# A causal attention's row maxima: the mask added by an identity matmul on TensorE instead of inside VectorE's reduction

## What is computed

```python
att = jnp.einsum('bhtd,bhsd->bhts', q, k) * scale
causal = jnp.tril(jnp.ones((T, T), dtype=bool))
att = jnp.where(causal, att, jnp.finfo(att.dtype).min)
att = jax.nn.softmax(att, axis=-1)
y = jnp.einsum('bhts,bhsd->bhtd', att, v)
```

## Time and profile before

| what | value |
|---|---|
| median of 3 runs | 748.03 us |
| lowest, highest | 746.31, 754.69 us |
| span of the profiled execution | 748.4 us |
| prologue of the causal attention | 287 to 317 us |
| its loop of eight steps | 317 to 622 us |
| last mixture of experts | 622 to 748.4 us |

### The profile page before, as it was taken

How to read it: one execution, slowest core, us unless ns; L and a number is a source line. 1 busy time by engine, 2 the same in 40 slices (tenths; PEclk the granted TensorE clock), 3 DMA queues, 4 the chain that set the end, 5 groups by cost and what they waited for, 6 DMA issues and landing times.

```text
span 748.4 us, 11770 instructions
## 1 busy us (share of the span) xinstructions
PE 666.3 (89%) x4108; PEld 456.7 (61%) x4108; DVE 501.7 (67%) x1560; ACT 356.8 (48%) x728; POOL 159.1 (21%) x290
## 2 busy tenths in 40 slices
PE   1875767899997997799998899999999997999998
PEld 1664656677776775465555555565555545777775
DVE  3578874776676648977665667769877425666654
ACT  3744355212222464166677678665666673222221
POOL 4563544330002430002433420203020000000000
PEclk9999989989999996799999999999999999999999
DMA  8000000000000000000000000000000000000000
GB/s 293 2 0 1 1 0 1 2 1 1 0 1 1 0 2 1 0 1 1 1 2 1 1 2 1 1 1 2 1 1 2 1 1 1 1 15 1 15 15 14
DMA packets 5722, 7.27 MB, mean 10 GB/s; under 512 B 416, under 2 KB 4640, under 8 KB 5664
## 3 DMA queue, kind: packets, MB, share of 16 engines
q1 hardware_dynamic: 4944, 4.59, 1.9%
q10 hardware_dynamic: 720, 1.93, 0.8%
HBM read 5.47 MB, written 1.05 MB: 9 GB/s over the span
## 4 chain that ended last, share of the span: by engine, by line
PE 70%; DVE 11%; ACT 4%; issue 3%; POOL 2%; POOLq 0%; ACTq 0%; DVEq 0%
PE bank L1568 12%; PE bank L1466 10%; PE bank L1596 10%; PE bank L1526 9%; PE bank L1251 6%; PE bank L1253 5%; PE bank L1252 5%; PE bank L1449 3%; PE bank L1578 2%; DVE hn L862 2%; DVE bank L1134 1%; DVE work L1137 1%; PE bank L1536 1%; PE bank L1259 1%; PE bank L1507 1%
## 5 line engine op out<-in xcount | busy, mean ns | idle before, releaser
L771 ACT ACTIVATE arena<-bank 128x512 f32<-128x512 f32 (+3 forms) x384 | 167.1, 493 | 88.7 <-PE bank L1578 65.1
L1134 DVE CUSTOM_DVE_ANT_0 bank<-bank,mask_qk 128x512 f32<-128x512 f32 (+3 forms) x256 | 121.2, 511 | 48.6 <-PE bank L1596 47.7
L1596 PE MATMUL bank<-kza,qta 128*128 128x512 f32 (+3 forms) x320 | 127.0, 410 | 5.7 <-DVE work L1134 2.0
L698 ACT ACTIVATE work<-bank 128x512 f32<-128x512 f32 x80 | 47.6, 597 | 171.7 <-PE bank L1449 171.7
L1568 PE MATMUL bank<-qtb,kza 128*128 128x512 f32 (+3 forms) x320 | 120.3, 388 | 2.0 <-ACT arena L771 1.0
L1061 DVE TENSOR_TENSOR work<-work,bank 128x512 f32<-128x512 f32 x80 | 54.9, 687 | 82.7 <-ACT work L698 82.2
L1137 DVE TENSOR_REDUCE work<-bank 128x1 f32<-128x512 f32 x128 | 81.6, 684 | 24.4 <-PE bank L1596 23.7
L1568 PEld LDWEIGHTS bank<-qtb,kza 128*128 128x128 f32 x320 | 60.5, 192 | 57.8 <-ACT arena L771 52.1
L1466 PE MATMUL bank<-dw,work 128*128 128x128 f32 x640 | 92.0, 288 | 0.1
L1466 PEld LDWEIGHTS bank<-dw,work 128*128 128x128 f32 x640 | 79.5, 195 | 11.5 <-issue 10.4
L1526 PE MATMUL bank<-arena 128*9 128x512 f32 (+3 forms) x768 | 80.1, 489 | 0.4 <-ACT arena L771 0.4
(11 more groups left out here) (200 smaller groups left out, 1166.0 us busy)
## 6 DMA issues: line engine op xcount, KB each, us to landing
x<-x_in SPq DMA_DIRECT2D x4, 256.0 KB, 10.1
y_out<-x SPq DMA_DIRECT2D x4, 256.0 KB, 2.3
arena<-const_in ACTq DMA_DIRECT2D x1, 976.0 KB, 8.0
arena<-gw_in SPq DMA_DIRECT2D x1, 640.0 KB, 9.2
arena<-uw_in SPq DMA_DIRECT2D x1, 640.0 KB, 8.4
dw<-dw_in SPq DMA_DIRECT2D x1, 640.0 KB, 9.4
work<-q_in SPq DMA_DIRECT2D x2, 256.0 KB, 6.9
arena<-wa_in ACTq DMA_DIRECT2D x1, 393.0 KB, 8.5
```

The costliest lines, as they stand in the source:

```text
L771: act.activation(pb[:, blk % 2, h, 0:w], s_bank(n)[:, 0:w], ACT.Exp, scale=SCALE).then_inc(p_ready, 1)
L1134: ins = dve.tensor_tensor_reduce(out=src, in0=src, in1=mask_qk[:, CW - w:], scale=1.0, scalar=-3e38, op0=ALU.add, op1=ALU.max, accum_out=dst)
L1596: pe.matmul(a_bank(n)[:, 0:w], qta[:, slot(b, g), i * P:(i + 1) * P], kz(s, h, half)[:, 0:w], start=True, stop=True).then_inc(a_full, 1)
```

## The change

Three edits. `mask_qk` shrinks from 512 columns (384 zeros and the triangle) to the 128 of the triangle, and the POOL memset of the zeros goes. On TensorE every masked `score_max` is followed by an identity matmul that accumulates `mask_qk` on the last 128 columns of the bank, and `a_full` is raised by that one. On VectorE all 384 maxima are a plain `tensor_reduce`.

```diff
-        mask_qk = sb("mask_qk", [P, CW], BF16)
+        mask_qk = sb("mask_qk", [P, P], BF16)
...
-            pool.memset(mask_qk[:, 0:CW - P], 0.0)
-            pool.tensor_copy(mask_qk[:, CW - P:], raw_c[:, C_MA:C_MA + P])
+            pool.tensor_copy(mask_qk[:, :], raw_c[:, C_MA:C_MA + P])
...
-                    if i * P < half * CW + w:
-
-                        ins = dve.tensor_tensor_reduce(out=src, in0=src, in1=mask_qk[:, CW - w:], scale=1.0,
-                                                       scalar=-3e38, op0=ALU.add, op1=ALU.max, accum_out=dst)
-                    else:
-                        ins = dve.tensor_reduce(dst, src, AX.X, ALU.max)
-                    ins.then_inc(a_free, 1)
+                    dve.tensor_reduce(dst, src, AX.X, ALU.max).then_inc(a_free, 1)
...
-                    pe.matmul(a_bank(n)[:, 0:w], qta[:, slot(b, g), i * P:(i + 1) * P],
-                              kz(s, h, half)[:, 0:w], start=True, stop=True).then_inc(a_full, 1)
+                    ins = pe.matmul(a_bank(n)[:, 0:w], qta[:, slot(b, g), i * P:(i + 1) * P],
+                                    kz(s, h, half)[:, 0:w], start=True, stop=True)
+                    if i * P < half * CW + w:
+                        ins = pe.matmul(a_bank(n)[:, w - P:w], identb[:, :], mask_qk[:, :], start=False, stop=True,
+                                        skip_group_check=True)
+                    ins.then_inc(a_full, 1)
```

## The result

The changed kernel takes 768.9 us (median of 4 runs, 767.45 to 770.26), the kernel before 747.17 us (median of 4, 745.78 to 754.69). The ratio is 1.0267, with a 95% interval of 1.0214 to 1.032. The forecast was 769.4 us, in a range of 761 to 777.

What follows compares the result with a forecast made beforehand. The prediction took DVE to bound the prologue and PE the loop. From 748.4 us it added 22.4 for masks on PE and took off 1 for gaps and 0.4 for the prologue: 769.4 us, range 761 to 777.

Steps and rivals of the forecast that it cites:

- The bound: Causal attention: DVE bounds the prologue (busy 29.55 of 30.00 us), PE the loop (292.59 of 305 us).
- The gain on DVE in the prologue: Plain instead of masked reductions gain about 0.05 us per maximum, 32 x 0.05 = 1.6 us in the prologue.
- the slope: Reductions on DVE fall 0.13 us per 128 columns, giving plain ones of 0.60, 0.47, 0.34 and 0.21 us.
- what PE would give back there: Prologue: added masks on PE at low clock offset DVE's 1.6 us gain; sum taken as -0.4 us.
- The bound of +2.9 us: Prologue's upper limit: PE at its low clock becomes the bound, and two runs of four blocks lose 2.9 us.
- Rival (d): Prologue: PE's denser work keeps or brings the higher clock, saving 2.6 us, time 766.8 us; chance 0.07.
- The price of a mask: Loop, PE: 0.12 us alone, 0.08 at 128 columns, 0.07 ahead of the sums; 22.4 us over seven steps.
- Rival (c): Each added mask on PE costs its whole row, 0.23 us, so 51.5 us more, about 798 us; chance 0.03.
- What falls in gaps: Loop: added matmuls fill PE's waits for exponentials and a maximum; 1 us taken off, between 0 and 12.4.
- The sum: Whole kernel: 748.4 + 22.4 - 1 - 0.4 = 769.4 us.
- (a): Loop: masks fall into PE's 12.4 us of idle time, leaving 10 us more, time 758 us; chance 0.05.
- (b): DVE sets the pace and shorter reductions pay everywhere, 12.8 us less, time 735.6 us; chance 0.02.

Runs made afterwards that it cites:

- e1: Changed kernel with TensorE's added masks kept but VectorE's old masked reduction put back (mask added twice): 770.22 us, ratio to before 1.0211.
- e2: Changed kernel with plain reductions but no mask for the maxima on either engine, second-pass masks zero (not causal): 748.25 us, ratio to before 0.9929.
- e8: The changed kernel repeated unchanged, with more rounds, beside the kernel before: 769.83 against 750.9 us, ratio 1.0237.
- e0: The kernel before, unchanged, profiled once more: median of one run 754.36 us, span 752.5 us.
- e7: Kernel before with the changed way only in the loop and the old way in the prologue: 775.82 us, ratio 1.029.
- e3: Changed kernel with each added identity matmul issued twice in a row: 777.93 us, ratio to before 1.0319.
- e6: Kernel before with the changed way only for the prologue's 32 masked maxima, the old way in the loop: 751.63 us, ratio 0.9993.
- e9: From e6, the second pass's third mask moved behind the score for the maxima, next to the sums: 750.01 us, ratio to before 0.9983.
- e5: Changed kernel with the added mask matmul streaming 256 columns instead of 128 where the block is wide enough: 771.37 us, ratio to before 1.0247.

## Why the prediction was right

**The bound.** Right for the loop. e1 and e2 part the change: the loop's cost comes with TensorE's matmuls and stays whether VectorE is relieved or not. VectorE's share was not quite nothing, 1.1 us in steps 1 to 6 (e2).

For the prologue it was right only in part. DVE is busy 29.55 of 30 us there, and yet the chain of the kernel before passes over PE for the scores of the first 12 maxima:

```profile
289.99 1.98 PE bank L1596 x3
...
292.02 2.04 PE bank L1596 x4
```

In the changed kernel it stays on DVE:

```profile
290.04 5.55 DVE work L1131 x12
```

The difference is the clock. The windows of the kernel before, of the changed kernel, and of the changed kernel again (e8):

```profile
292.00:297.00 5.00, 4.35 (x13) 3.14 (x13) 4.85 (x21) 1.40 (x3) 0.00 (x0) 0.50 0.00 0
...
293.00:298.00 5.00, 4.26 (x25) 3.14 (x24) 4.97 (x15) 1.36 (x3) 0.00 (x0) 0.99 0.00 0
...
293.00:298.00 5.00, 4.74 (x22) 3.86 (x22) 4.43 (x13) 1.44 (x3) 0.00 (x0) 0.50 0.00 0
```

**The gain on DVE in the prologue.** The 0.05 us a maximum, and the slope by which I had guessed the narrow reductions, hold. The chain of the changed kernel has the last twelve, of 384, 256 and 128 columns:

```profile
311.79 3.99 DVE work L1131 x12
```

The forecast's slope gives 4 x (0.47 + 0.34 + 0.21) = 4.1 us. From the 13th maximum on, DVE alone sets the pace: 20.3 us to the loop's first score in the four profiles with the old reductions there (before, e0, e1, e7), 19.35 us in all others but e3 (19.66), 0.96 us for 20 masked maxima.

The term that was mis-sized is what PE would give back there. I took -0.4 us as the sum, and it was -2.0 (e8: -1.2, e6: -1.8). Most of the rest of it, beside those 0.96 us, comes in the first 12 maxima, from the first reduction to the 13th. They take 7.45 us before and 6.61 us in the changed kernel, where PE has the higher clock. At the lower one PE does set their pace: 7.24 us with the masks (e8) and 7.07 us without them and with plain reductions (e2), so the masks cost 0.17 us there. The bound of +2.9 us had PE as the slower in both runs of four masked blocks; even in e8 it was so in the first only.

The clock is the part that I had wrong. Rival (d), to which I gave 0.07, has this mechanism. Of the nine profiles with masks in the prologue eight had a granted clock of 0.99 or 1.00 in such a window, and of the four without them none (0.50 in each). e8 is the ninth, so the masks don't bring it every time, and no run tried what does.

**The price of a mask.** Right: 0.07 and 0.05 us, and 0.07 ahead of the sums. A wide block was put at 0.43 us and a narrow one at 0.31; between neighbouring sums, where nothing else moved, the one grew by 0.36 to 0.47 and the other by 0.26 to 0.35. That the narrow ones grew by less fits the third score's wait for VectorE, which is gone (e9). A step without waits, step 3, went from 37.68 to 40.85 us: 3.17 against 3.20 in the forecast. Rival (c) fell with e3 and e5. The trace is also above the 81 ns of the Trainium skill (TensorE: Matmul & The Clock Gate, Back-to-back issue gap) for a mask that stands alone among fp32r loads, at 0.12 us, and below it, at 0.055 us, for one in a run of masks.

**What falls in gaps.** This is the other mis-sized term. The loop grew by 18.6 us, and seven clean steps would be 7 x 3.17 = 22.2. I had taken 1 us off; 3.6 us came off. Step 4 grew by 2.38 and step 5 by 2.71 us, 1.2 us less than two clean ones. There the chain of the kernel before goes over VectorE for some 4 us, and the changed kernel's stays on PE:

```profile
514.40 0.97 DVE hn L862 x4
515.37 0.34 DVE bank L1134
```

Steps 1 and 2 together grew by 4.1 us, 2.2 less than two clean ones, and most of that is not idle time that was filled. It is a fall of the clock that is gone. Before, at 395 us:

```profile
395.00:400.00 5.00, 3.96 (x18) 1.78 (x17) 2.28 (x6) 2.83 (x5) 0.00 (x0) 0.66 0.01 3
```

The same place after, some 5 us later:

```profile
395.00:400.00 5.00, 5.00 (x51) 3.55 (x50) 2.57 (x8) 3.98 (x12) 4.08 (x9) 1.00 0.00 0
400.00:405.00 5.00, 3.97 (x28) 2.36 (x28) 2.49 (x4) 3.40 (x6) 0.00 (x0) 1.00 0.00 0
```

A mean of 0.66 over 5 us means 1.7 us lost at half clock. PE was busy 3.97 of 5 us after as it was 3.96 before, and kept 2.4 GHz. This is the mechanism of rival (d) once more, but not where (d) had put it: at the loop's start the clock was low in both.

**The sum.** The loop was put 2.8 us too high and the prologue 1.6 too high. That the forecast still lies 0.5 us from the median is partly luck: the base of 748.4 us was a span, to be raised by 1.85 us, and the parts that the change doesn't touch added 2.3 us in the profiles. Against e8 the forecast of 21.0 us is 3 us above the 17.8 measured.

**Rivals (a) and (b).** PE's idle time stayed at 13.0 us, so (a) fell. e2 gives (b) 1.1 us in steps 1 to 6, where it needed 192 x 0.05 = 9.6.

## What to carry to other kernels

Where TensorE sets the pace, work moved to it from an engine that waits is paid nearly in full, even in the smallest of matmuls. Price such a matmul by what the chain of waits shows for it and for the one behind it, not by its row: here 0.12 us against 0.23. Its place matters as much as its number: the 224 masks of the loop cost 19.0 us where three of four stood alone ahead of a full weight load, and 5.5 us where they stood in runs or ahead of a matmul with a small load. (The 5.5 us include a mask of the second pass that the new order moved too, and both are against a kernel before that lost 1.7 us to a fall of its clock.)

A busy share near 1 does not show that an engine is the bound: DVE was at 29.55 of 30 us in the prologue while the chain went over PE. And a row of waits shows only waits in which the engine is seen idle; one that a running matmul covers is found by comparing the end of what it needs with its own start.

## What the runs showed that I had not expected

A mask of 256 columns between two matmuls that need full weight loads was no dearer than one of 128 (e5); ahead of the sums, with their small load, it was.

Behind its first microseconds the loop had a fall of the clock, to a mean of 0.66 to 0.72 over 5 us, once in each of the four profiles that have neither the added masks in the loop nor a new order (before, e0, e2, e6), and in none of the other nine. The place differs: 395 to 405 us in the first two, 440 to 450 us in e2 and e6. In e6 it is this window:

```profile
440.00:445.00 5.00, 4.48 (x21) 2.38 (x22) 2.39 (x7) 2.51 (x5) 0.00 (x0) 0.66 0.00 0
```

What decides it was not tried.
